# A transformer decoder layer: the output projection of the last stage in f16 parts

## The reference

```python
def layer(x, ctx, seq_mask):
    x = x + self_attention(layernorm(x))        # 16 heads, two sets of keys and values, mixed; ends in "out @ Wo"
    x = x + cross_attention(ctx, layernorm(x))  # 8 heads; keys and values are the halves of ctx
    return x + ffn(layernorm(x))                # down(silu(gate(h)) * up(h))

def ffn(h):                                     # every operand goes through fp4_quant_dequant first
    gate, up = fp4_linear(h, w_gate), fp4_linear(h, w_up)       # 512 -> 1408
    return fp4_linear(silu(gate) * up, w_down)                  # 1408 -> 512
# fp4_quant_dequant: blocks of 16; scale = max|x| / 6; x / scale is put on the grid 0, .5, 1, 1.5, 2, 3, 4, 6
```

## Time and profile before

| | us |
|---|---|
| median of three runs | 4969.36 (4959.97 to 4973.95) |
| the profiled execution | 4962.72 |
| its span, first to last instruction | 4960.9 |
| the span up to the last stage's first load | 3859.97 |
| the last stage | 1100.93 |
| in it: TensorE / VectorE / ScalarE / GpSimd busy | 1024.86 / 879.94 / 555.15 / 356.89 |
| in it: mean granted TensorE clock | 0.96 of full speed |
| in it: the projection's matmuls, 256 records | 129.9 busy, 29.3 idle before them |

### The profile page before, as it was taken

One profiled execution on the slowest core, in us unless ns is written; L12 is line 12 of the kernel. 1 busy time (PEld: TensorE's weight loads), 2 busy tenths in 40 slices (PEclk: granted clock), 3 DMA queues, 4 the chain that ended last, 5 costly groups with the idle time before them and its releaser, 6 DMA issues. The chain is left out here.

```text
span 4960.9 us, 101557 instructions
## 1 busy us (share of the span) xinstructions
PE 4775.8 (96%) x31276; PEld 2094.0 (42%) x31276; DVE 4041.5 (81%) x6609; ACT 2998.4 (60%) x5234; POOL 3020.0 (61%) x1271
## 2 busy tenths in 40 slices
PE   8998999999999999999999999999998699999998
PEld 3444333333333333333333333333332477777776
DVE  7567888888888888888888888888884488888887
ACT  3222476777777777777777767677766355555554
POOL 0000488888878878787887888888778133333332
PEclk9999799999999999999999999999999699999999
DMA  5444476776777767677676776767766100000000
GB/s 172 122 142 137 103 171 171 169 175 171 170 174 167 175 170 171 171 168 179 167 171 167 171 176 168 174 167 171 177 148 148 66 23 27 27 27 27 27 22 12
DMA packets 216979, 661.84 MB, mean 133 GB/s; under 512 B 38099, under 2 KB 111955, under 8 KB 158997
## 3 DMA queue, kind: packets, MB, share of 16 engines
q0 software_dynamic: 64512, 469.79, 40.8%
q1 hardware_dynamic: 151919, 185.58, 12.4%
q10 hardware_dynamic: 38, 0.08, 0.0%
HBM read 123.56 MB, written 61.64 MB: 37 GB/s over the span
## 5 line engine op out<-in xcount | busy, mean ns | idle before, releaser
L885 DVE TENSOR_REDUCE rowmax_parts<-scores_qk 128x1 f32<-128x512 f32 x4096 | 2525.4, 679 | 475.4 <-PE scores_qk L958 475.4
L869 ACT ACTIVATE probs_T<-scores_kq 128x512 f32<-128x512 f32 x4096 | 2286.3, 596 | 985.4 <-PE scores_kq L958 916.4
L802 POOL TENSOR_TENSOR probs_added<-probs_added,probs_T 128x2048 f32<-128x2048 f32 x448 | 2030.8, 4533 | 461.9 <-ACT probs_T L869 450.6
L958 PE MATMUL scores_kq<-q_operand,k_operand 103*128 103x512 f16 (+3 forms) x3712 | 1274.6, 349 | 10.2 <-ACT probs_T L869 8.3
L958 PE MATMUL scores_qk<-k_operand,q_operand 96*128 96x512 f16 (+4 forms) x3712 | 1121.6, 351 | 39.9 <-DMA v_operand<-v_dram 14.8
L1029 PE MATMUL outputs_T<-probs_T,v_operand 128*32 128x512 f32 x8192 | 1092.6, 605 | 1.3 <-ACT probs_T L869 1.3
L958 PEld LDWEIGHTS scores_kq<-q_operand,k_operand 103*128 103x128 f16 x3712 | 358.7, 97 | 920.3 <-ACT probs_T L869 635.3
L958 PEld LDWEIGHTS scores_qk<-k_operand,q_operand 96*128 96x128 f16 (+1 forms) x3712 | 354.6, 98 | 433.9 <-DVE rowmax_parts L885 185.0
L1636 PE MATMUL f_gate_up<-w_gate_up,xq_T 128*128 128x256 f16 (+1 forms) x4608 | 494.2, 266 | 8.6 <-DVE hidden L1527 7.5
L1636 PEld LDWEIGHTS f_gate_up<-w_gate_up,xq_T 128*128 128x128 f16 x4608 | 421.4, 99 | 77.8 <-issue 25.4
L802 POOL TENSOR_TENSOR probs_added<-probs_T 128x2048 f32<-128x2048 f32 x64 | 290.3, 4536 | 233.8 <-ACT probs_T L869 233.8
(11 more groups left out here) (165 smaller groups left out, 4291.8 us busy)
## 6 DMA issues: line engine op xcount, KB each, us to landing
probs_poured<-probs_T POOLq DMA_DIRECT2D x448, 1024.0 KB, 7.2
qk_parts_dram<-qk_parts SPq DMA_DIRECT2D x96, 256.0 KB, 2.9
q_operand<-qk_parts_dram SPq DMA_DIRECT2D x192, 128.0 KB, 2.6
k_operand<-qk_parts_dram SPq DMA_DIRECT2D x192, 128.0 KB, 3.2
v_dram<-v_heads SPq DMA_DIRECT2D x16, 1024.0 KB, 6.4
v_operand<-v_dram SPq DMA_DIRECT2D x64, 256.0 KB, 6.2
q_operand_above<-qk_parts_dram SPq DMA_DIRECT2D x96, 128.0 KB, 2.8
x_groups<-x SPq DMA_DIRECT2D x8, 1024.0 KB, 9.5
```

Source lines behind the costliest of these rows:

```text
L802: nc.gpsimd.tensor_tensor(total, first, probs[:, b % PBUF, :], ALU.add).then_inc(added.sem, 1)
L869: nc.scalar.activation(probs[:, kb % PBUF, qt * BANK:(qt + 1) * BANK], pb[:, k % 2, :], ACT.Exp)\
L885: nc.vector.reduce_max(rowmax[:, w % 2, c // NQ, c % NQ:c % NQ + 1], pa[:, k % 3, :], AX.X)\
L958: return nc.tensor.matmul(out, lhsT, rhs, start=start, stop=stop, skip_group_check=True)
```

## The change

`Wo` is split once, at the start of the stage: ScalarE writes the high part of 64 x Wo in f16 (`wo_parts[:, 0]`), VectorE the remainder (`wo_parts[:, 1]`). The attention's outputs are split for every tile by two new steps: `high attn` on ScalarE copies the tile to f16, and `low attn` on GpSimd subtracts that from the float32 tile. Both work two tiles ahead of the turn's own, in one buffer of two parts. `project` then has twelve f16 matmuls for the four in float32, and `measure out` multiplies the sum by 1/64 while it adds x. The wait for the load moves from TensorE to `high attn`; `project` waits for `low attn` in its place, and the first one for the split of Wo.

```diff
 ORDER_ACT = (
...
-    ("silu4", -1), ("silu5", -1), ("high x", 0), ("copy xT", 0), ("exp", 1), ("copy probs", 1), ("high h0", -1),
+    ("silu4", -1), ("silu5", -1), ("high attn", 2), ("high x", 0), ("copy xT", 0), ("exp", 1), ("copy probs", 1),
...
 ORDER_POOL = (
-    ("add cross", 0), ("low h1", -2), ("divide x", 0), ("round x", 0), ("low x", 0), ("low h0", -1),
+    ("add cross", 0), ("low h1", -2), ("divide x", 0), ("round x", 0), ("low x", 0), ("low attn", 2),
...
+        wo_parts = sb("wo_parts", [P, 2, KT, H], F16)
+        aT_parts = sb("attn_T_parts", [P, 2, KT, P], F16)
...
         def _(pool):
...
+                if kind == "low attn":
+                    a_hi.passed(pool, n)
+                    nc.gpsimd.tensor_tensor(aT_parts[:, 1, :, :], aT[:, n % 2, :, :], aT_parts[:, 0, :, :], ALU.subtract)\
+                        .then_inc(a_lo.sem, 1)
...
         def _(act):
+            act.wait_ge(weights, 64)
+            nc.scalar.activation(wo_parts[:, 0, :, :], wo_sb[:, :, :], ACT.Copy, scale=UPSCALE).then_inc(wo_hi, 1)
             act.wait_ge(ready, 3)
...
+                if kind == "high attn":
+                    got[n % 2].passed(act, n // 2)
+                    o_product.passed(act, n - 1)
+                    nc.scalar.copy(aT_parts[:, 0, :, :], aT[:, n % 2, :, :]).then_inc(a_hi.sem, 1)
...
         def _(dve):
...
+            dve.wait_ge(wo_hi, 1)
+            nc.vector.scalar_tensor_tensor(wo_parts[:, 1, :, :], wo_sb[:, :, :], UPSCALE, wo_parts[:, 0, :, :],
+                                           ALU.mult, ALU.subtract).then_inc(wo_lo, 1)
...
-                    nc.vector.tensor_tensor(x1[:, n % 2, :], pl[:, 0, :], xt[:, n % 2, :], ALU.add).then_inc(summed1.sem, 1)
+                    nc.vector.scalar_tensor_tensor(x1[:, n % 2, :], pl[:, 0, :], 1.0 / UPSCALE, xt[:, n % 2, :],
+                                                   ALU.mult, ALU.add).then_inc(summed1.sem, 1)
...
                 if kind == "project":
-                    got[n % 2].passed(pe, n // 2)
+                    if n == 0:
+                        pe.wait_ge(wo_lo, 1)
+                    a_lo.passed(pe, n)
                     x_scaled.passed(pe, n - 1)
                     for c in range(KT):
-                        last = nc.tensor.matmul(pl[:, 0, :], aT[:, n % 2, c, :], wo_sb[:, c, :], start=c == 0, stop=c == KT - 1)
+                        for a, b in PRODUCTS:
+                            last = nc.tensor.matmul(pl[:, 0, :], aT_parts[:, a, c, :], wo_parts[:, b, c, :],
+                                                    start=c == 0 and a == b, stop=c == KT - 1 and a == 1)
```

More of the change, by code:

```diff
@@ L1137 @@
     ("silu2", -1), ("silu3", -1), ("copy hT 1", -2), ("norm out", 1), ("copy hT 2", -2), ("copy q", 1),
-    ("silu4", -1), ("silu5", -1), ("high x", 0), ("copy xT", 0), ("exp", 1), ("copy probs", 1), ("high h0", -1),
-    ("silu1", 0),
+    ("silu4", -1), ("silu5", -1), ("high attn", 2), ("high x", 0), ("copy xT", 0), ("exp", 1), ("copy probs", 1),
+    ("high h0", -1), ("silu1", 0),
 )
 ORDER_POOL = (
-    ("add cross", 0), ("low h1", -2), ("divide x", 0), ("round x", 0), ("low x", 0), ("low h0", -1),
+    ("add cross", 0), ("low h1", -2), ("divide x", 0), ("round x", 0), ("low x", 0), ("low attn", 2),
+    ("low h0", -1),
 )
@@ L1245, in finish @@
         M = lambda name, per=1, step=1: Mark(sem("f_" + name), per, step)
+        wo_hi, wo_lo = sem("f_wo_hi"), sem("f_wo_lo")
         weights, wd_in, k_turned, k_copied, mask_link, ident0, ready = (sem("f_" + k) for k in
@@ L1252, in finish @@
         shifted = [M(f"shifted{i}") for i in range(2)]
+        a_hi, a_lo = M("attn_hi"), M("attn_lo")
         o_product, summed1, q_turned, q_copied = M("o_product"), M("x1"), M("q_turned"), M("q_copied")
@@ L1316, in slot @@
             def slot(kind, n):
-                if kind == "add cross":
+                if kind == "low attn":
+                    a_hi.passed(pool, n)
+                    nc.gpsimd.tensor_tensor(aT_parts[:, 1, :, :], aT[:, n % 2, :, :], aT_parts[:, 0, :, :], ALU.subtract)\
+                        .then_inc(a_lo.sem, 1)
+                elif kind == "add cross":
                     x_scaled.passed(pool, n)
@@ L1374, in slot @@
             def slot(kind, n):
-                if kind == "warm silu":
+                if kind == "high attn":
+                    got[n % 2].passed(act, n // 2)
+                    o_product.passed(act, n - 1)
+                    nc.scalar.copy(aT_parts[:, 0, :, :], aT[:, n % 2, :, :]).then_inc(a_hi.sem, 1)
+                elif kind == "warm silu":
                     warm(0, ACT.Silu)
```

## The result

The changed kernel takes 4984.77 us (median of 6 runs, 4983.35 to 4985.62); the kernel before takes 4965.42 beside it (6 runs, 4959.97 to 4973.95). The ratio is 1.0035, with a 95% interval of 1.0024 to 1.0047: 0.35% slower. The profiled span went from 4960.9 to 4983.1. Of these 22.2 us, 21.9 were lost in the last stage (1122.8 us from its first load to the end, against 1100.9), and 0.3 ahead of it.

The account below looks back on a forecast made before the run. A loop over TensorE and VectorE was taken to bound each last-stage tile. Steady tiles -1, clock falls +20 and the start -2 made +17 on the profiled 4962.7: 4979 us, range 4943 to 4998.

Parts of the forecast that it names:

- Projection: Last stage, each tile: twelve f16 products take 2.59 us where four f32 took 3.51, saving 0.92 on the loop.
- "low attn": GpSimd's subtraction in each tile makes VectorE's L112, in the first-half quantisation, lose 0.82 us (bounds 0 and 1.45).
- "high attn": ScalarE's f16 cast in each tile, right ahead of the cast of x, costs the loop 0.09 us.
- Steady tiles: Last stage, per tile: -0.92 + 0.09 + 0.82 = -0.01 us, taken as -0.03 over 28 tiles, -1 us.
- The clock: TensorE's wait before the projection grows to 1.8 us: 12 more falls at 1.69 each, +20 us (0 to 42).
- The start: Last stage's start: first projection 3.6 us later but shorter, next three tiles save 4; taken as -2 (-5 to +3).
- The rivals: GpSimd fits beside VectorE, 4935 to 4944, 17%; clock stays up, 4957 to 4965, 20%; falls nearly everywhere, 4991 to 5003, 18%.

## Why the prediction was right

4979 was forecast (the sum, 4962.7 + 17, is 4979.7), within 0.3% of no change, and 4984.77 measured. The steps, by the profiled executions (+17 forecast, +22.2 measured):

- **Projection.** Twelve records, and 2.58 from their start to the next group's (2.59 forecast); the saving of 0.92 is confirmed by the tile of 31.00 with the steps moved.
- **"low attn".** 0.84 on L112, where 0.82 was forecast, by the order of service that was forecast: "low attn" ends 1.02 after L111, and L112 0.81 after that (1.01 and 0.81 forecast). The second half shows a move that wasn't forecast and costs nothing: "low h0" now meets L112 (2.28) where it met L113 (2.25 in the earlier trace rows). The Trainium skill, "SBUF — State Buffer", "Who interferes with whom", says that the one issued second is fully blocked. The trace agrees that the two wait for each other when both read, but not on the price: 0.84, where the prediction's estimate for a whole instruction was 1.11.
- **"high attn".** 0.09 was forecast and it is 0. The step rested on the cast starting only when silu has ended. ScalarE after shows it starting 0.14 before that (4370.89 + 0.57 = 4371.46, against 4371.32):

```profile
4370.89 0.57 ACT L1445 ACTIVATE silu<-f_gate_up 128x256 f32<-128x256 f32 x2
4371.32 0.64 ACT L1389 CAST attn_T_parts<-attn_T 128x512 f16<-128x512 f32 x1
4371.98 0.62 ACT L1423 CAST x_parts<-x_quantised 128x512 f16<-128x512 f32 x1
```

- **Steady tiles.** Forecast -0.03 x 28 = -1; it is -0.06 in each, -1.5 over 25.
- **The clock, the term that was too small.** The wait is 1.78 (1.8 forecast), a fall costs 1.69 (as forecast), and they are 17 in 25 tiles, 19 in the forecast's 28 (15 forecast): in the 25, 14 more than before x 1.69 = +23.7 instead of +20. The granted clock in the last stage is 0.94 (0.93 forecast). The middle between no and every tile was a choice, not a reading, and it came near by luck: nothing in the trace of before told 8 from 21.
- **The start.** -2 was forecast, and it is +0.4, 0.3 of it lost ahead of the stage. The first projection, to set beside the earlier trace rows, comes 3.57 later (3.6 forecast) and is done in 4.27 (5.2 forecast; the mean granted clock is 0.64 in it, 0.55 before):

```profile
3875.25 4.27 PE L1584 MATMUL f_logits<-wo_parts,attn_T_parts 128*128 128x512 f16 x12 [4.23 <-POOL attn_T_parts L1324]
```

So the first x_out is 1.03 late (2.1 forecast). The failed part is the -4 given to the next three tiles because they had "no first-half quantisation to be held up": that holds for one of them, which wins 0.83 back. The tile behind it, from the x_out at 3927.94 on, already has one, as VectorE's timeline shows, and it wins 0.18. The next three come to -0.07, +1.63 (a fall) and -1.18, which makes the 0.4:

```profile
3945.60 1.79 DVE L111 TENSOR_TENSOR hidden_q<-hidden_q,f_m 128x768 f32<-128x768 f32 x1
3947.43 1.79 DVE L112 TENSOR_TENSOR hidden_q<-hidden_q,f_m 128x768 f32<-128x768 f32 x1
```

The rivals' times hold in the kernels built for them: 4935.35 where GpSimd's work doesn't meet the quantisation (4935 to 4944), 4953.7 where it does and the clock stays up (4957 to 4965, which counts 3 to 6 falls; here no steady tile falls).

What stays open: why two tiles in three fall, and what TensorE has to do ahead of a wait for the clock to stay. The runs vary the wait and the work ahead of it together.

## What to carry to other kernels

A step that is put into another engine's idle time can cost that engine's neighbour time at SBUF, though the idle time is real: look at what the neighbour does at that moment, and move the step to a place where that engine isn't lengthened. Reading a single tensor isn't proof against it: in the earlier trace rows L109, which reads one, took 1.30 beside GpSimd's L1336, and L110 0.56. A saving on one engine of a two-engine loop that the other can't use comes back as idle time, and idle time of TensorE may cost its clock. Before a splitting is judged by its time, try its steps in two or three places: here the place was worth 49 us, more than the projection's whole saving.

## What was not expected of the hardware

- A write-only GpSimd operation of 1.12 us ran beside two VectorE instructions that read two tensors, and lengthened neither, as that run's theory had it.
- Work that nobody needs made kernels faster: four products in the wait brought 31 us in the changed kernel, 7.6 in the kernel before, and about 7 with the steps moved.
- The slow tiles come in a regular pattern: two of three after, six of eight with the f32 projection and the same wait.
- A ScalarE instruction's record starts up to 0.14 us ahead of the end of the one before it, so a cast of 0.64 fitted where the rows showed a gap of 0.53.
